# A transformer block with routed experts on one core: router weights carried in the scattered rows, one expert prepared early, plain stores for the last two steps

## The reference

```python
x = x + layernorm(attention(layernorm(x)))     # S = g*S + k v^T ; y = q S, then Wo
x = x + layernorm(ffn(layernorm(x)))
# ffn, with 8 experts and the 2 best of them for each row:
gate_out = x @ gate_w                          # 8 logits a row
w = softmax over the two largest logits, 0 elsewhere
out = sum_e swiglu(x, ew1[e], ew2[e], ew3[e]) * w[:, e] + swiglu(x, sw1, sw2, sw3)
swiglu(x, w1, w2, w3) = (silu(x @ w1) * (x @ w2)) @ w3      # hidden size 512
```

## Time and profile before

| | us |
|---|---|
| median of 3 runs | 833.86 (831.44 to 841.46) |
| the profiled execution | 839.79, its span 837.9 |
| busy in the span: PE | 732.9 |
| DVE | 551.6 |
| POOL | 507.4 |
| ACT | 408.4 |

### The profile page before, as it was taken

The page is one execution under the profiler, slowest core; times in us unless marked ns, Lnnn a source line. Parts: engine busy times, 40 slices in busy tenths (PEclk is TensorE's granted clock), DMA queues, the critical chain, the costliest instruction groups (busy, mean ns, idle before and its releaser), DMA issues. The chain is left out here.

```text
span 837.9 us, 25066 instructions
## 1 busy us (share of the span) xinstructions
PE 732.9 (87%) x8863; PEld 609.9 (73%) x8863; DVE 551.6 (66%) x1130; ACT 408.4 (49%) x793; POOL 507.4 (61%) x672
## 2 busy tenths in 40 slices
PE   5889988898999878287999999999999999998970
PEld 4677776776877766165878999999999866887750
DVE  4999999888998886375777544444444434468852
ACT  3656655555666653222334444444444445445551
POOL 4133346776687676578098877886663444258864
PEclk9999999899999999587999999999999999999995
DMA  7435333443335433796212221212222122148864
GB/s 250 103 79 123 91 116 88 145 116 116 116 118 143 122 114 107 247 310 229 62 27 52 65 77 59 60 51 91 77 84 58 53 65 66 56 134 177 179 147 50
DMA packets 56934, 92.70 MB, mean 111 GB/s; under 512 B 7184, under 2 KB 35216, under 8 KB 56816
## 3 DMA queue, kind: packets, MB, share of 16 engines
q1 hardware_dynamic: 39424, 59.61, 25.4%
q0 software_dynamic: 11216, 23.10, 10.1%
q10 hardware_dynamic: 6176, 8.40, 3.1%
HBM read 59.07 MB, written 32.01 MB: 109 GB/s over the span
## 5 line engine op out<-in xcount | busy, mean ns | idle before, releaser
L1260 PE MATMUL bank<-xh,W 128*128 128x256 f16 x1504 | 261.8, 275 | 20.0 <-DVE gl L1556 13.8
L1260 PE MATMUL bank<-xl,W 128*128 128x256 f16 x752 | 206.8, 275 | 3.3 <-issue 3.3
L1260 PEld LDWEIGHTS bank<-xh,W 128*128 (+1 forms) x1504 | 148.2, 99 | 47.0 <-issue 16.7
L1301 PE MATMUL bank<-W,gh 128*128 (+1 forms) x824 | 142.3, 277 | 5.8 <-DVE gl L1556 3.9
L1339 ACT ACTIVATE gh<-bank 128x512 f16<-128x512 f32 x103 | 61.4, 596 | 160.8 <-DVE bank L1565 146.6
L1641 POOL DMA_INDIRECT yt_scratch<-ysh,dest x71 | 77.0, 1085 | 101.4 <-ACT ysh L1374 60.2
L1556 DVE TENSOR_TENSOR gl<-bank,gh 128x512 f16<-128x512 f32 x103 | 71.1, 691 | 73.0 <-ACT gh L1339 65.0
L1301 PE MATMUL bank<-W,gl 128*128 (+1 forms) x412 | 114.2, 277 | 0.0
L544 POOL DMA_INDIRECT xs_scratch<-xn_all,posi x64 | 92.9, 1451 | 27.5 <-issue 15.3
L1565 DVE SCALAR_TENSOR_TENSOR bank<-sl,w_scale,bank 128x512 f32<-128x512 f32 x94 | 70.9, 754 | 56.7 <-PE bank L1260 42.4
L596 PE MATMUL bank<-xnT,wT 128*128 128x256 f32 x384 | 93.6, 395 | 2.3 <-ACT xnT L371 2.3
(11 more groups left out here) (200 smaller groups left out, 1330.6 us busy)
## 6 DMA issues: line engine op xcount, KB each, us to landing
W<-gate_scratch SPq DMA_DIRECT2D x64, 256.0 KB
ysh<-yt_scratch SPq DMA_DIRECT2D x16, 512.0 KB, 4.4
xt<-xs_scratch SPq DMA_DIRECT2D x31, 260.0 KB
W<-in_L_ffn_ew_dram ACTq DMA_DIRECT2D x15, 512.0 KB, 3.8
W<-in_L_ffn_ew_dram SPq DMA_DIRECT2D x9, 512.0 KB, 9.1
x_in<-in_L_attn_x_dram SPq DMA_DIRECT2D x16, 256.0 KB, 4.0
out_dram<-x SPq DMA_DIRECT2D x16, 256.0 KB
xT_scratch<-xn2T SPq DMA_DIRECT2D x16, 256.0 KB
```

The source lines that it names most:

```text
L1260: last = mm(dst[n % 2][:, i * R:(i + 1) * R], W16[:, e, m, s, at:at + P], a[:, k, :], start=(k == 0 and s == 0 and a is x_h), stop=(k == K ...
L1301: last = mm(pYB[t.u % 2][:, r * D:(r + 1) * D], g[:, i, r, :], W16[:, e, 2, s, c * D:(c + 1) * D], start=(c == 0 and r == 0 and a is gh an ...
```

## The change

Six things are done together.

1. The router's weights travel with the rows. In attention DVE takes the difference of the two best logits a step (`dv`), ACT makes tanh(dv/2) of it straight into column D + 3 of xn2 (`share`), and POOL makes column D + 2 (`scatter` has one more small instruction and one more wait). With routed units, DVE computes each row's factor (weight times the expert's scale) in `weights_of_rows`: a register read of the next unit's expert, three linked instructions and a fourth, on 128 x 2 elements. ACT's eviction uses it, one instruction a tile where there was one a unit. `wts_all` and what made it are gone, and so are POOL's two multiplications in mixing and DVE's.
2. Expert 1 is split by POOL in attention, a matrix (1024 elements a partition) at the end of each of the iterations 5, 6 and 7, through two slots of the xn2 ring. `split` in the expert part starts with expert 2.
3. EARLY is 4. So one shared unit moves from before the routed ones to behind them, T0 is 44, and the 14 steps of mixing are spread over 9 units, two in five of them.
4. The table is made in five parts, in gaps (0,0) to (1,1) and no longer in unit 0's three; `turn` becomes `3 * u + gap - 5`, so that every maximum and both scales come two gaps later. ACT loads one matrix where it loaded two.
5. In mixing DVE adds the shared result behind `gated(t, 0)`, steps are normed a unit later, there are three `lnc` buffers, and at the seam from singles to shared units PE projects the single ahead of the hidden products.
6. Steps 14 and 15: DVE takes the shared result straight from PSUM, adds x1 (loaded again at unit T0 + 2) itself, and SP stores with plain transfers.

The rows' loads (L1196) now wait for `weights_of_rows` of the unit two before, where they waited for ACT's tags.

```diff
-    EARLY = 5
+    EARLY = 4
@@ scalar_a
+            def share(s):
+                act.wait_ge(s_dv, s + 1)
+                act.activation(xn2[s % XB][:, :, D + 3], dv[:, s], ACT.Tanh, scale=0.5).then_inc(s_share, 1)
@@ pool_a, scatter
+                pool.wait_ge(s_share, s + 1)
                 pool.tensor_copy(xn2[s % XB][:, :, D:D + 2], tag_all[:, s]).then_inc(S["tag_ready"], 1)
+                pool.tensor_scalar(xn2[s % XB][:, :, D + 2], xn2[s % XB][:, :, D + 3], -0.5, 0.5, ALU.mult, ALU.add)\
+                    .then_inc(S["tag_ready"], 1)
@@ pool_a
+            def split_first(m):
+                pool.wait_ge(s_scale, 1)
+                link(pool.tensor_scalar(spare_rows, W[:, 1, m, :], w_scale[:, 1, 1:2], 1.0, ALU.mult, ALU.mult))
+                link(pool.tensor_copy(W16[:, 1, m, 0, :], spare_rows))
+                last = pool.tensor_tensor(W16[:, 1, m, 1, :], spare_rows, W16[:, 1, m, 0, :], ALU.subtract)
...
                 on(residual, i - 2)
+                if 0 <= i - SPLIT - 1 < 3:
+                    split_first(i - SPLIT - 1)
@@ vector_a, top
+                V.tensor_tensor(dv[:, s], mx[:, s, :, 1], mx[:, s, :, 0], ALU.subtract).then_inc(s_dv, 1)
@@ sync_b, load
-                    need(sp, T["tag_ready"], 2 * (t.q - 1))
+                    need(sp, T["wrow_ready"], t.q - 1)
@@ scalar_b, rows_out
+                if t.routed:
+                    act.wait_ge(T["wrow_ready"], t.q + 1)
+                    for r in range(t.tiles):
+                        act.activation(ysh[:, ETILES + (t.j + r) % RING, :], pYB[t.u % 2][:, r * D:(r + 1) * D], ACT.Copy,
+                                       scale=wrow[:, t.j + r:t.j + r + 1]).then_inc(T["yo_ready"], 1)
@@ vector_b
-                turn = 3 * u + gap - 3
+                turn = 3 * u + gap - TABLE          # TABLE = 5
+            def weights_of_rows(t, e):
+                x = xt[t.q % 2]
+                own, part, out = chosen2[:, 0, 0:t.tiles], chosen2[:, 1, 0:t.tiles], wrow[:, t.j:t.j + t.tiles]
+                dve.wait_ge(T["tag_ready"], 2 * (t.q + 1))
+                link(V.tensor_scalar(own, tag[:, t.j:t.j + t.tiles, 1], 0.0, None, ALU.is_equal))
+                link(V.tensor_tensor(part, own, x[:, 0:t.tiles, D + 3], ALU.mult))
+                link(V.tensor_tensor(part, part, x[:, 0:t.tiles, D + 2], ALU.add))
+                V.tensor_scalar(out, part, w_scale[:, 2, e], None, ALU.mult).then_inc(T["wrow_ready"], 1)
@@ vector_b, loop
-                if steps:
-                    if steps[0] > 0:
-                        shift(steps[0] - 1)
-                    add_rows(steps[0])
+                if following is not None and following.routed:
+                    weights_of_rows(following, expert_of(dve, following))
+                if waiting is not None:
+                    shift(waiting)
                 beside(u, 0)
                 if t is not None:
                     e = expert_of(dve, t)
                     gated(t, 0, e)
                 if steps:
+                    add_rows(steps[0])
                     stats_of(steps[0])
@@ pool_c, add_first
-                for b in range(B):
-                    pool.tensor_scalar(cmb[:, c % MIXED, b, :], ya[c % 2][:, b, 0, :], wts_all[:, c, b, 0:1], 1.0,
-                                       ALU.mult, ALU.mult).then_inc(U["weighed"], 1)
-                pool.wait_ge(U["weighed"], B * (c + 1))
-                pool.tensor_tensor(cmb[:, c % MIXED], cmb[:, c % MIXED], ysh[:, B * c:B * (c + 1), :], ALU.add)\
+                pool.tensor_tensor(cmb[:, c % MIXED], ya[c % 2][:, :, 0, :], ya[c % 2][:, :, 1, :], ALU.add)\
                     .then_inc(U["mix1"], 1)
@@ the last two steps
+                if c in PLAIN:
+                    dve.wait_ge(T["y_done"], shared[c].u + 1)
+                    V.scalar_tensor_tensor(a, pYB[shared[c].u % 2][:, :], w_scale[:, 2, 0:1], a, ALU.mult, ALU.add)\
+                     .then_inc(U["mix2"], 1)
...
+                    V.tensor_tensor(lnc[c % LN][:, b, :], lnc[c % LN][:, b, :], x1_of[c][:, b, :], ALU.add)\
+                     .then_inc(U["sum_ready"], 1)
...
+                sp.dma_start(out_by_step[c], lnc[c % LN][:, :, :]).then_inc(last_stored, 16)
```

More of the change, by code:

```diff
@@ L1132, in sandwich_kernel, with rows_upto @@
         tile_unit = {t.j + r: t for t in routed for r in range(t.tiles)}
+        def rows_upto(u):
+            return sum(t.tiles if t.routed else 1 for t in units[:u + 1])
         def halves_upto(u):
@@ L1314, in tensor_b @@
                     turn_x(following)
+                late = [y for y in projected(u) if y.kind == "single" and t is not None and t.kind == "shared"]
+                for y in late:
+                    project(y, e_of.pop(y.u))
                 if t is not None:
@@ L1387, in load_matrices @@
             def load_matrices():
-                for e, m in [x for x in (next(matrices, None), next(matrices, None)) if x]:
+                e, m = next(matrices, (None, None))
+                if e is not None:
                     load_matrix(act, e, m)
@@ L1646, in pool_b @@
             j = 0
-            for n, (first, end) in enumerate(GROUPS):
+            for n, (first, end) in list(enumerate(GROUPS))[1:]:
                 pool.wait_ge(s_scale, n + 1)
-                for e in range(max(first, 1), end):
+                for e in range(first, end):
                     split(e)
```

181 lines of the change are left out of this document (108 added, 73 removed).

## The result

| | before | after |
|---|---|---|
| device time, median (lowest to highest) | 835.82 us (831.44 to 841.46) | 867.84 us (867.42 to 868.87) |
| runs | 4 | 4 |
| span of the profiled execution | 837.9 us | 865.9 us |
| granted clock over the span | 0.953 | 0.942 |

The ratio is 1.0381, with a 95% interval from 1.0313 to 1.0449: the changed kernel is slower by 32 us, outside the predicted range of 812 to 852.

What follows compares the result with a forecast made beforehand. PE and DVE nearly fill attention, PE bounds routed units, DVE four units behind the seam. Terms 4 - 13.3 + 7.9 + 11.6 + 7 + 4 + 1 - 10 - 10 = +2.2 us on 833.86 give 836, range 812 to 852.

Steps and rivals of the forecast that it cites:

- e: Splits of experts 2 to 4 behind the seam: two DVE weights_of_rows calls wait for POOL's instructions, +7 us (0 to 16).
- f: Splits of experts 5 to 8: DVE's calls wait for POOL, 4.7 us of slack, one us each, +4 us (0 to 15).
- rival 3: Splits of experts: all four DVE instructions wait one POOL instruction each, 9 to 14 us a call; 861 us, chance 0.12.
- a: Expert 1's splits in attention: POOL's time is free, but its instructions hold up DVE, +4 us (nothing to 11.6).
- b: Seam after attention: the first pair's rows come sooner, PE waits 9 us and turns it earlier, -13.3 us.
- c: One more shared unit behind the routed ones, +7.9 us.
- h: Tail units: less POOL and DVE work a step, fewer doubles, a third buffer removing waits, -10 us (-4 to -13).
- d: Behind the seam, to the eighth pair: DVE's later maxima and added work delay expert 2, +11.6 us (+6 to +15).
- g: Single routed units: weights_of_rows and its register take 1.45 of 1.5 us in hand, +1 us (0 to 3).
- The last unit: Last tail unit, to the end of the last matmul: its wait for DVE shrinks, -2 us, counted within the tail's -10.
- i: Drain from the last matmul to the end: 10 us instead of 20.1, -10 us (-8 to -11).
- the lock: In POOL's splits of experts 2 to 8, DVE's SBUF-only weights_of_rows instructions wait for POOL instructions to end, +7 and +4 us.

Runs made afterwards that it cites:

- e1: Changed kernel with the four small DVE instructions of weights_of_rows as tensor_reduce of the same size (row weights wrong, time only): 836.7 us, 1.000 of before.
- e8: Changed kernel with POOL splitting experts 2 to 8 a third at a time, nine instructions of 1024 elements instead of three of 3072: 845.7 us.
- e5: e4 without the split of expert 1 in attention; POOL splits it behind the last scatters, as before: 826.6 us, 0.989 of before.
- e4: e2 with EARLY 5, so five shared units ahead of the routed ones as in before: 835.3 us, 0.997 of before.
- e15: e5 run again, unchanged, beside a later group: 824.5 us.
- e16: e4 run again, unchanged, beside a later group: 832.2 us.
- e2: Changed kernel with the rows' weights worked out on ACT and nothing of it on DVE: 835.8 us, 1.001 of before.
- e11: e4 with the split of expert 1 in attention in quarters, twelve instructions of 256 elements a step (expert 1's matrices wrong): 852.3 us.
- e12: e5 with POOL writing zeros, four times 1024 elements, at the three places of the attention split: 829.1 us, two runs.
- e3: Kernel before with DVE's weights_of_rows added, result unused, the rows' load behind it: 874.2 us, 1.049 of before.
- e9: Changed kernel with the first three weights_of_rows instructions as reductions (weights wrong), only the last tensor_scalar kept: 847.8 us.
- e10: e5 with ACT and DVE both taking the first pair's x at the end of the unit ahead: 827.6 us, 0.983 of its before.
- e13: e4 with the attention split moved up in POOL's step, ahead of a wait of POOL: 829.6 us.
- e14: e12 run again: e5 with POOL writing zeros at the places of the attention split: 830.7 us, eight runs.
- e6: e4 with DVE converting the first pair's x at the end of the unit ahead, not at its start: 837.0 us.
- e7: e5 with DVE converting the first pair's x at the end of the unit ahead, not at its start: 825.4 us, 0.988 of its before.

## Why the prediction was wrong

**The step that failed: e and f, "So one call waits for two ends of POOL instructions, 5 to 8 us".** The mechanism was named, with its place (experts 2 to 4, then 5 to 8), but the forecast took it at 11 us together. It is 31 to 32: 31.1 between the medians of after and e1, 16.7 + 15.4 between their marks. The working had two of the four instructions slip through. In the two calls shown only the chain's second slips; the first, third and fourth are held and take 2.2, 5.8 and 2.8 us or 2.7, 2.6 and 5.9. Between the third and the fourth POOL's next instruction has started (438.98 against 439.05). The three calls that start in the splits of experts 2, 4 and 5 take 11.2, 11.7 and 11.4 us, where a free one takes 0.95. That is what rival 3 had ("9 to 14 us a call"), and so are its sizes, +16 and 15 for e and f. That rival, put at 0.12, is what happened in e, and nearly its time, 861; that its 15 for f fits is luck, since only one of the four calls there was a long one. The prediction had the evidence: it put "some 0.1 us" between two POOL instructions and about 0.2 on each link. In such a gap one link can start, as L1594 does, but not two.

The Trainium skill (SBUF — State Buffer, "Who interferes with whom") says that copies, casts and tensor_scalar can take the port pair that GpSimd uses, that a DVE instruction with two SBUF inputs contends with a GpSimd one that reads SBUF, that the holder keeps the pair for a whole instruction, and that tensor_reduce never contends on this chip. The runs agree in each point: 5.95 us for L1596, a tensor_scalar of two elements; 5.86 for L1595, with two inputs; 0.157 at most for the reductions of e1. Of this the prediction named the part on two inputs, and let all four instructions meet POOL's; what a call pays was worked out too small.

**f, the slack, "DVE may lag 4.7 us".** The calls at the splits of experts 5 to 8 took 10.4, 5.6, 6.3 and 5.5 us more than a free one, three of them within the forecast's 5 to 8. The pairs around them, 8.3 us apart otherwise, lost 8.7, 1.5, 4.0 and 1.4 us (from the marks of ACT). So 1.7 to 4.1 us of a call were hidden, not 4.7, and half of f is the one long call. In e8, with calls of 2 to 4 us, the stretch is 192.8 us, 2.0 above before. That a short wait is hidden holds; its bound was put too high.

**a, +4.** e5 against e4, and e15 against e16, have it at 7.9 and 7.6 us, with five shared units ahead. The step that failed: "POOL's time is free". POOL is idle for 106 of 280 us, but not behind residual, where the split was put: the roots for ACT are next in its order. One profiled execution didn't show it. In the nine kernels with the split or the zeros in attention (without e2, e11 and e12) the last pad scatter started at 387 to 398 us, on average at 391.8; in the six without, at 379 to 388, on average at 384.1: 7.7 us apart, where the pair in hand had 3.2 (389.26 against 386.08).

**b, -13.3.** The size is near, the mechanism is not the one forecast. From the start of the last pad scatter to PE's first turn it is 21.3 us in before and 22.2 in e3, and 8.2 to 9.0 in after, e1, e8 and e9: 12 to 14 less. But the forecast had PE ready by about 385, waiting 9 us for the rows. It was not ready before 398: it crawls from 382 to 394, then works up to the turn. What moved the turn is one shared unit less to do. The rows were there sooner as well, but with five units ahead that gains nothing, as e4 shows. And that a and b together came out at -9.2 against -9.3 is luck in part. With attention as in after, PE's first turn was at 398.2, 407.5 (e1), 398.3 (e8) and 402.2 us (e9); with attention as in before, at 407.4 and 401.3 (e3). On average that is some 3 us sooner, not 9. The load of expert 2's first pair and the scales at 427 came as forecast. **c, +7.9; h, -10.** Together -0.1 forecast without the last unit, +1.9 measured; a tail unit takes 8.1 us (89.5 for eleven), near the 8.2 foretold. **d, +11.6.** By e1 it is 15.2; the mechanism (maxima behind the seam) was right, as POOL's 36.87 us of waiting for the scales and e10's 5 us show, the size 3.6 us short. **g, +1.** -0.3. **The last unit, -2.** -3.3. **i, -10.** -8.7. The timeline of SP of after has the last store, which has replaced the accumulating one of the earlier trace rows:

```profile
861.83 0.38 SPq L1251 DMA_DIRECT2D out_dram<-lnc  x1
```

The span ends 4.1 us behind its start; the forecast had given 3.7 us to the store, issue and end, and 6.3 from the last matmul to it, where it took 7.3.

**Without the lock** the forecast would have been 9 us below before; e1 and e2 are 0.4 and 1.3 below theirs. So some 8 us were missing there as well. d (3.6), c and h (2) and a (about 4) are enough for it, but how they add up in a median run was not measured.

## What to carry to other kernels

A chain of tiny DVE instructions that runs beside GpSimd's long ones costs not its own time but the rest of one GpSimd instruction for as many as three of four links (11 us for four links here); price a call so, and only then take off the slack. Three ways out were measured: another engine (e2), a kind of instruction that isn't held up (e1), shorter GpSimd instructions (e8: 22 of the 31 us; in attention the same step made it worse, e11). An engine's idle time is not free at every place of its program: look at what stands right behind the insertion, and who waits for that (e5 against e4; e13, where a third of the cost came back). A sum that comes out right, like a and b here, can hide a cost too small and a wait that never was; look for the wait itself in the trace. And a single profiled execution can't price a term of a few us in a stretch whose end wanders by 8 (e4 and e16 are the same kernel, with the last pad scatter at 395.3 and 387.2 us): count from the last mark before the part that matters, as for e10. e5, which has the weights on ACT, no split in attention and five shared units ahead, is 1.1% faster than before (826.6 us, 0.989 [0.985, 0.993]), and the cost of the split that it leaves out could not be read off the profiles of before and after.

## What the runs showed of the hardware

- A tensor_scalar of 128x2 with one SBUF input took 5.95 us beside a GpSimd subtraction of 128x3072, and a copy of 128x8 took 1.97 us beside one of 128x1024; reductions of 128x2 or 128x1 never more than 0.157 us (e1, 160 of them). Beside GpSimd's writing of zeros, 128x1024, a copy of 128x8 took 0.97 us (e14).
- In a split GpSimd's next instruction starts about 0.1 us after the last, and a chain on DVE with 0.03 to 0.15 us between its links is held again and again: 11.2 and 11.7 us for four instructions.
- In the profile of after PE's granted clock was 0.87 from 100 to 180 us, where POOL's splits stand, and PE was busy 66.55 us of the 80; before it was 0.94 and 72.33. The two windows:

```profile
100.00:180.00 80.00, 66.55 (x1034) 53.09 (x1033) 73.88 (x152) 41.19 (x81) 54.95 (x71) 0.87 0.31 92
```
```profile
100.00:180.00 80.00, 72.33 (x1257) 57.72 (x1258) 72.47 (x164) 47.97 (x90) 46.49 (x73) 0.94 0.38 107
```

The figures are shares of the full clock, 2.4 GHz, averaged over stretches at either level. In the same window the granted clock is 0.87 to 0.91 in e1, e4, e6, e8, e9, e14 and e16, which have the split or the zeros at that place, 0.94 to 0.98 in e3, e5, e7, e10 and e15, which have neither, and 0.96 in e13. Whether PE's pauses or the lower clock came first, and how much of term a the clock carries, was not measured by itself.
